# Graph convolution stage on one core: pairs of 64-row products replaced by 128-row products, and four buffers behind the first product

## The chip, the cores and the metric

The kernel runs on 1 core of one Trainium2 chip (trn2). The metric is the device time of one execution in microseconds (us), lower is better. The kernel before takes 10347.91 us, the median of 3 runs (10343.13 to 10349.23).

## The reference, cut to what matters

Four graph layers follow one another on 100000 nodes and 50000 edges with 64 features. The change touches the first layer alone, two "tag convolutions" in a row:

```python
K = 5;  F_IN, F_HID, F_OUT = (64, 128, 64)

def _tag_conv(x, row, col, norm, W, b):
    out = x @ W[0]
    h = x
    for k in range(1, K + 1):
        msg = h[row] * norm[:, None]
        h = jax.ops.segment_sum(msg, col, num_segments=N_NODES)
        out = out + h @ W[k]
    return out + b

h = jax.nn.leaky_relu(_tag_conv(x, row, col, norm, W0, b0), negative_slope=0.01)
h = jax.nn.leaky_relu(_tag_conv(h, row, col, norm, W1, b1), negative_slope=0.01)
```

`W0` is 6 x 64 x 128 and `W1` is 6 x 128 x 64. So for each row of a node that receives edges the first convolution needs six products (x and its five hops, 64 features each) that are added into 128 hidden features, and the second begins with one product of these 128 by all six matrices of `W1` side by side (6 x 64 = 384 columns). The other three layers (a SAGE and GAT layer, a GCN layer, a GAT layer with a dense one) are not touched.

## The kernel before, in words

Edges are sorted by target. They are laid out as 128 partitions by 392 columns, and worked on in NG = 49 groups of 8 columns; a group holds 1024 rows of 64 float32, 256 KB. The first layer runs in four parts. (1) The rows of x are gathered into the table `xc`. (2) Four hop stages: GpSimd (POOL) gathers 8 columns of rows per group, one indirect DMA each (`gather`, L710), VectorE (DVE) weighs them (`feed_vector`, L739) and forms running sums in a ring of three buffers `sums` (L753, L763), SyncE (SP) stores them as the next hop's table. Beside it TensorE (PE) transposes each group into feature-major form, ScalarE (ACT) copies the result (L1056), and SP stores it in the "turned" tables, so that four of the six operands of the first convolution lie in DRAM already turned. Layers for nodes without edges ("dense") run beside these stages and are spread over them by step numbers. (3) The **conv stage**, which the change is about, with no dense work in it: the fifth hop (called `top`) is gathered and summed in the same way, and both the first convolution and the product by `W1` are computed group by group. (4) Five "up" stages, which gather rows of the results y5 to y0 and so form the second convolution.

The order of the conv stage is written out by hand, engine by engine, for a group g:

- SP: `cat_load(g)` (L1286, L1289) loads x from `xc` and the four turned tables into `cat[g % 2]`, five transfers of 256 KB, once the products of group g-2 are done. `y_store(g - 3)` (L1295) then stores six blocks of 256 KB.
- PE, `conv_tensor`: `conv_turn(g, 0)` transposes x (four 128x128 transposes, L1079), `conv_turn(g, 1)` the sums. A partition of such a turned block is 64 features of one column (rows 0 to 63) and 64 of the next (rows 64 to 127). `conv_mult` (L1095) does six steps of two products, each over 64 partitions, 64x128 weights and 512 columns: one for the upper and one for the lower half, into the banks PS[2] and PS[3]. The first waits for `biased`, that is until ACT has emptied these banks from group g-1. Then `conv_out(g - 1)` does 8 products (L1108, 128 partitions by 384 columns) into three banks in turn; product y waits until bank y-3 has been copied out.
- ACT, `conv_scalar`: two copies of transposed blocks (`conv_move`, L1128), then the four even copies out of the product banks (`conv_out_scalar(g - 1)`, L1139), then the bias, two activations (L1156) from PS[2] and PS[3] into the two buffers `hid`. They wait for the products of the first convolution and, since `hid` has two buffers alone, for all 8 products of `conv_out(g - 1)`.
- DVE: `feed_vector(g)`, 8 steps of sums (`paced_sums`), then the four odd copies (`conv_out_vector(g - 3)`, L1146), then the leaky relu of two buffers (`conv_leak(g - 2)`, L1162).
- POOL gathers up to six groups ahead of DVE.

The waits that the change moves are these (L1151 to L1156):

```python
if g:
    conv_out_scalar(e, g - 1)
e.wait_ge(*conv["mult"](K6 * (g + 1)))
e.wait_ge(*conv["product"](K8 * g))
for a in range(2):
    e.activation(hid[a][:, :], PS[2 + a][:, :], ACT.Identity,
```

## Time and profile before

| | |
|---|---|
| time, median of 3 runs | 10347.91 us (10343.13 to 10349.23) |
| the profiled execution: its time, its span | 10350.19 us, 10348.5 us |
| PE busy / weight loads | 5760.6 us (56%) / 2887.3 us (28%) |
| DVE busy | 5897.1 us (57%) |
| ACT busy | 3169.7 us (31%) |
| POOL busy | 6886.8 us (67%) |
| DMA | 1016.84 MB, 98 GB/s on average |
| mean granted TensorE clock | 0.768 |

The busy shares are averages over stages with different limits. PE counts two instructions per float32 product, and for each a weight load that can run beside the product before it. The granted clock is 1.00 at 2.4 GHz and 0.50 at 1.2 GHz. The conv stage runs from about 3205 to 3846 us of the span. How the page and the answers are read: each row of a timeline begins with the start and the length in us, and in brackets stand the idle time of the engine before it and what released it.

### The profile page before, as it was taken

To read this page: it belongs to the slowest core of one execution; us is meant where nothing else is said; L and a number is where in the kernel's file an instruction comes from. 1 tells how busy PE (TensorE), PEld (TensorE's weight loads), DVE (VectorE), ACT (ScalarE), POOL (GpSimd) and SP (SyncE) were. 2 spreads that over 40 slices of the span, in tenths; PEclk is the share of its full clock that TensorE was granted. 3 is DMA by queue.
4 is the path that set the end of the run, shared out by engine and by line. 5 is a ranking of instruction groups with operands and counts; after the bars stand their busy time and mean duration, and the time that the engine had idled before them with its cause. 6 is when DMAs were issued, how large, how long until landed. Compare 5 with 4: busy or idle time off the path is not lost. (4 is left out here: it accounts for less than half of the span.)

```text
span 10348.5 us, 86417 instructions
## 1 busy us (share of the span) xinstructions
PE 5760.6 (56%) x19261; PEld 2887.3 (28%) x19261; DVE 5897.1 (57%) x16861; ACT 3169.7 (31%) x5395; POOL 6886.8 (67%) x6659
## 2 busy tenths in 40 slices
PE   1672465555566984555555400598885776720277
PEld 0331232333333542222222200243222333410143
DVE  2341565556555656666666578544449994520697
ACT  0351233333332322222222201244443553310144
POOL 7777777777777747777777777775750006767477
PEclk9796677777777996676666655799998997755698
DMA  4620332222224752222222222222333442222353
GB/s 130 202 84 20 84 109 89 89 86 92 87 90 156 245 206 83 89 88 85 86 89 86 82 74 80 69 72 57 72 61 111 146 139 63 75 52 52 81 151 121
DMA packets 967572, 1016.84 MB, mean 98 GB/s; under 512 B 530229, under 2 KB 584231, under 8 KB 954507
## 3 DMA queue, kind: packets, MB, share of 16 engines
q1 hardware_dynamic: 754186, 880.78, 26.3%
q0 software_dynamic: 212864, 130.53, 7.1%
q8 instruction: 154, 2.52, 0.1%
q14 instruction: 368, 3.01, 0.1%
HBM read 491.86 MB, written 596.27 MB: 105 GB/s over the span
## 5 line engine op out<-in xcount | busy, mean ns | idle before, releaser
L710 POOL DMA_INDIRECT gathered<-u,place_of_source x1564 | 1645.0, 1052 | 522.5 <-issue 476.3
L710 POOL DMA_INDIRECT gathered<-hop,place_of_source x1564 | 1615.0, 1033 | 530.4 <-issue 492.0
L763 DVE SCALAR_TENSOR_TENSOR first_node_sum<-sums,ends_first,first_node_sum 128x64 f32<-128x64 f32 x4680 | 1302.7, 278 | 8.3 <-DVE sums L753 6.8
L739 DVE TENSOR_TENSOR weighted<-gathered,bank 128x512 f32<-128x512 f32 (+1 forms) x490 | 335.6, 685 | 1407.5 <-DMA gathered<-hop,place_of_source 625.3
L753 DVE SCALAR_TENSOR_TENSOR sums<-sums,same_as_before,weighted 128x64 f32<-128x64 f32 x3900 | 1079.3, 277 | 69.0 <-DVE weighted L739 41.9
L710 POOL DMA_INDIRECT gathered<-x,row_of_source x782 | 806.3, 1031 | 300.0 <-issue 224.0
L480 PE MATMUL bank<-dense_tmp,mean 128*128 128x512 f32 x980 | 569.5, 684 | 37.4 <-ACT dense_tmp L489 31.7
L2187 POOL DMA_INDIRECT out_dram<-lane_out,node_to_write x392 | 407.2, 1039 | 274.5 <-ACT lane_out L2108 160.2
L710 POOL DMA_INDIRECT gathered<-y,place_of_source x391 | 406.8, 1040 | 233.0 <-issue 118.9
L710 POOL DMA_INDIRECT first_sum<-head_sums,row_of_first_end x2 | 2.0, 1025 | 827.9 <-DMA head_sums<-head_sums 827.6
L710 POOL DMA_INDIRECT pair<-h_sage,row_of_source x391 | 404.6, 1035 | 220.5 <-issue 125.6
L459 PE MATMUL bank<-g3pair,dense_yT 128*128 128x16 f32 x784 | 176.1, 304 | 669.2 <-DVE dense_yT L529 669.2
L710 POOL DMA_INDIRECT source_row<-x,row_of_source x391 | 398.6, 1019 | 155.1 <-issue 118.9
L480 PE MATMUL bank<-dense_a,center 128*128 128x512 f32 x588 | 406.3, 781 | 168.5 <-DVE dense_a L504 116.8
L710 POOL DMA_INDIRECT gathered<-in_x_dram,dst_index x392 | 401.2, 1024 | 130.0 <-issue 116.5
L710 POOL DMA_INDIRECT gathered<-x_with_place,src_index x391 | 401.4, 1027 | 120.8 <-issue 118.3
L1030 POOL DMA_INDIRECT x_with_place<-own_place,place_to_write x391 | 396.9, 1015 | 127.2 <-issue 127.2
L491 ACT ACTIVATE dense_a<-bank,v_bl 128x512 f32<-128x512 f32 x196 | 134.7, 687 | 1075.8 <-PE bank L602 860.2
L459 PEld LDWEIGHTS bank<-g3pair,dense_yT 128*128 128x128 f32 x784 | 185.6, 311 | 747.9 <-DVE dense_yT L529 747.9
L2227 DVE SCALAR_TENSOR_TENSOR head_sums<-head_sums,same_as_before 128x256 f32<-128x256 f32 x780 | 379.4, 486 | 22.7
L423 PE MATMUL bank<-ident,dense_xT 128*128 128x128 f32 x392 | 96.6, 393 | 510.1 <-DVE dense_xT L529 510.1
L491 ACT ACTIVATE dense_tmp<-bank,eps_col 128x512 f32<-128x512 f32 x490 | 336.3, 687 | 142.8 <-PE bank L480 141.2
(446 smaller groups left out, 15158.6 us busy)
## 6 DMA issues: line engine op xcount, KB each, us to landing
head_sums<-head_sums SPq DMA_DIRECT2D x98, 1024.0 KB, 4.7
y<-conv_out SPq DMA_DIRECT2D x294, 256.0 KB
conv_out<-y SPq DMA_DIRECT2D x245, 256.0 KB, 3.3
hop<-sums SPq DMA_DIRECT2D x196, 256.0 KB, 2.1
turned<-rows_turned SPq DMA_DIRECT2D x196, 256.0 KB, 2.7
cat<-turned SPq DMA_DIRECT2D x196, 256.0 KB
u<-conv_out SPq DMA_DIRECT2D x196, 256.0 KB, 2.0
lane_raw<-x SPq DMA_DIRECT2D x196, 256.0 KB
```

Source lines behind the costliest of these rows:

```text
L423: m = e.transpose(W.bank[l][0][:, q * P:(q + 1) * P], src_ap(l, q), ident[:])
L459: e.matmul(W.bank[l][1][:, q * 4 * HEADS:(q + 1) * 4 * HEADS], two, wts[w][:], start=True, stop=True)
L480: m = e.matmul(W.bank[l][b][:, :], w, W.b(v, l), start=i == 0, stop=i == len(pairs) - 1)
L491: m = e.activation(W.b(o, l), src_ap, func, bias=v[:, 0:1], scale=scale)
L710: return e.indirect_dma_start(out=into, out_offset=None, in_=tab, in_offset=bass.IndirectOffsetOnAxis(ap=index, axis=0), bounds_check=top, ...
L739: e.tensor_tensor(weighted[g % 2][:, 0:n, :], st.rows_of(g), over(st.weight[:, cols], D), ALU.mult).then_inc(st.weighed.handle, 1)
L753: e.scalar_tensor_tensor(s[:, k, :], b, go[:, t:t + 1], m[:, k, :], ALU.mult, ALU.add).then_inc(st.summed.handle, 1)
L763: e.scalar_tensor_tensor(h, row_, flast[:, t:t + 1], h, ALU.mult, ALU.add).then_inc(st.headed.handle, 1)
L1030: e.indirect_dma_start(out=x66, out_offset=bass.IndirectOffsetOnAxis(ap=place_at[:, t:t + 1], axis=0), in_=own[:, t, :], in_offset=None, b ...
L2187: e.indirect_dma_start(out=out, out_offset=bass.IndirectOffsetOnAxis(ap=scat[:, t:t + 1], axis=0), in_=W.out[0][0][:, k * D:(k + 1) * D], ...
L2227: e.scalar_tensor_tensor(s[:, k, :], b, go[:, t:t + 1], s[:, k, :], ALU.mult, ALU.add).then_inc(summed.handle, 1)
```

## The change

1. The operands of the first product are laid so that a column of 128 partitions holds two tables (hop 1 and 2; hop 3 and 4; x and hop 5) for the same rows: `TWO`, weights `w0two` (three 128x128 blocks). `conv_mult` has three steps of two products over 128 partitions.
2. To get this layout, the turned tables are one DRAM tensor, of which `cat_load` takes four pieces of 64 partitions; x is loaded into `both[g % 3]`, beside the sums of `top`, row for row, so that one set of 8 transposes turns both.
3. `hid` has four buffers; ACT's bias stands ahead of the copies of `conv_out(g - 1)` and waits for `conv_out(g - 2)` alone; DVE does the leaky relu of g-1 right behind the sums of g, and the copies of g-2 behind it.

```diff
-            cat = [sb(ctx, f"cat{i}", [P, HOPS, 512]) for i in range(2)]
-            hid = [sb(ctx, f"hidden{i}", [P, 512]) for i in range(2)]
+            both = [sb(ctx, f"x_and_sums{i}", [P, K8, 2, D]) for i in range(3)]
+            top_sums = [a[:, :, 1, :] for a in both]
+            cat = [sb(ctx, f"cat{i}", [P, 2, 2, 512]) for i in range(2)]
+            hid = [sb(ctx, f"hidden{i}", [P, 512]) for i in range(4)]
...
-            def conv_turn(e, g, i):
-                n = 2 * g + i
-                if i:
-                    e.wait_ge(*top.ended(g))
-                else:
-                    e.wait_ge(*cat_in[g % 2](16 * HOPS * (g // 2 + 1)))
-                if n >= 2:
-                    e.wait_ge(*conv["moved"](n - 1))
-                two = sums[g % 3][:].rearrange("p k d -> p (k d)") if i else cat[g % 2][:, 0, :]
+            def conv_turn(e, g, a):
+                if a == 0:
+                    e.wait_ge(*x_again[g % 3](16 * (g // 3 + 1)))
+                    e.wait_ge(*top.ended(g))
+                if g:
+                    e.wait_ge(*conv["moved"](2 * g + a - 1))
                 for q in range(4):
-                    t = e.transpose(PS[i][:, q * P:(q + 1) * P], two[:, q * P:(q + 1) * P], ident[:])
+                    t = e.transpose(PS[a][:, q * P:(q + 1) * P], both[g % 3][:, 2 * q + a, :, :].rearrange("p s d -> p (s d)"), ident[:])
                 t.then_inc(conv["turned"].handle, 1)
...
-                    half = slice(a * D, (a + 1) * D)
-                    t = e.matmul(PS[2 + a][:, :], wts["w0pair"][half, k, :], rhs[half, :], start=m == 0, stop=m == HOPS)
+                    n = 2 * g + a
+                    if m == 2:
+                        e.wait_ge(*conv["moved"](n + 1))
+                    rhs = turned_t[n % 4][:, :] if m == 2 else cat[g % 2][:, m, a, :]
+                    t = e.matmul(PS[2 + a][:, :], wts["w0two"][:, m, :], rhs, start=m == 0, stop=m == 2)
...
-                for m in range(HOPS + 1):
+                for m in range(3):
                     conv_mult(e, g, m)
...
+                e.wait_ge(*conv["mult"](3 * (g + 1)))
+                if g >= 2:
+                    e.wait_ge(*conv["product"](K8 * (g - 1)))
+                for a in range(2):
+                    e.activation(hid[2 * (g % 2) + a][:, :], PS[2 + a][:, :], ACT.Identity,
+                                 bias=wts["v_b0"][:, 0:1]).then_inc(conv["biased"].handle, 1)
                 if g:
                     conv_out_scalar(e, g - 1)
-                e.wait_ge(*conv["mult"](K6 * (g + 1)))
-                e.wait_ge(*conv["product"](K8 * g))
-                for a in range(2):
-                    e.activation(hid[a][:, :], PS[2 + a][:, :], ACT.Identity,
-                                 bias=wts["v_b0"][:, 0:1]).then_inc(conv["biased"].handle, 1)
...
+                    tables = turned.rearrange("(m s g a f) c -> s g f m a c", m=2, s=2, g=NG, a=2)
                     def cat_load(g):
+                        if g >= 3:
+                            e.wait_ge(*conv["turned"](2 * (g - 2)))
+                        e.dma_start(both[g % 3][:, :, 0, :], columns(xc, g)).then_inc(x_again[g % 3].handle, 16)
                         if g >= 2:
-                            e.wait_ge(*conv["mult"](K6 * (g - 1)))
-                        e.dma_start(cat[g % 2][:, 0, :].rearrange("p (k d) -> p k d", d=D), columns(xc, g)
-                                    ).then_inc(cat_in[g % 2].handle, 16)
-                        for m in range(1, HOPS):
-                            e.dma_start(cat[g % 2][:, m, :], ttab[m - 1][g * P:(g + 1) * P, :]).then_inc(cat_in[g % 2].handle, 16)
+                            e.wait_ge(*conv["mult"](3 * (g - 1)))
+                        for m in range(2):
+                            for s in range(2):
+                                e.dma_start(cat[g % 2][s * D:(s + 1) * D, m, :, :], tables[s, g, :, m, :, :]).then_inc(cat_in[g % 2].handle, 16)
...
-                        paced_sums(e, top, g, sums[g % 3], sums[(g - 1) % 3], none, 0, 0, False)
-                        if g >= 3:
-                            conv_out_vector(e, g - 3)
+                        paced_sums(e, top, g, top_sums[g % 3], top_sums[(g - 1) % 3], none, 0, 0, False)
+                        if g:
+                            conv_leak(e, g - 1)
                         if g >= 2:
-                            conv_leak(e, g - 2)
-                    conv_out_vector(e, NG - 3)
-                    conv_leak(e, NG - 2)
-                    fix_vector(e, top, sums[(NG - 1) % 3])
+                            conv_out_vector(e, g - 2)
+                    fix_vector(e, top, top_sums[(NG - 1) % 3])
+                    conv_leak(e, NG - 1)
                     conv_out_vector(e, NG - 2)
-                    conv_leak(e, NG - 1)
                     conv_out_vector(e, NG - 1)
```

ACT in the middle of the conv stage, one group, before (`rows_turned` are the copies of transposed blocks, `conv_out` the copies out of the product banks):

```order
L1128 COPY rows_turned_1<-bank 128x512 [waits conv_mult,conv_turned] x2
L1139 COPY conv_out_1<-bank 128x6x64 [waits conv_product,y_stored1]
L1139 COPY conv_out_1<-bank 128x6x64 [waits conv_product] x3
L1156 ACTIVATE hidden_1<-bank,v_b_1 128x512 [waits conv_product,conv_mult]
L1156 ACTIVATE hidden_1<-bank,v_b_1 128x512
```

and with the change:

```order
L1129 COPY rows_turned_1<-bank 128x512 [waits conv_mult,conv_turned] x2
L1156 ACTIVATE hidden_1<-bank,v_b_1 128x512 [waits conv_product,conv_mult]
L1156 ACTIVATE hidden_1<-bank,v_b_1 128x512
L1140 COPY conv_out_1<-bank 128x6x64 [waits conv_product,y_stored1]
L1140 COPY conv_out_1<-bank 128x6x64 [waits conv_product] x3
```

The two activations moved from behind the four copies to ahead of them.

DVE there, from the end of one group's sums to the beginning of the next, before:

```order
L763 SCALAR_TENSOR_TENSOR first_node_sum<-sums_1,ends_first,first_node_sum 128x64 [waits first_added,summed]
L1146 COPY conv_out_1<-bank 128x6x64 [waits conv_product,y_stored0]
L1146 COPY conv_out_1<-bank 128x6x64 [waits conv_product] x3
L1162 SCALAR_TENSOR_TENSOR hidden_1<-hidden_1 128x512 [waits conv_biased] x2
L739 TENSOR_TENSOR weighted_1<-gathered_1,bank 128x512 [waits gathered0]
```

and with the change:

```order
L765 SCALAR_TENSOR_TENSOR first_node_sum<-x_and_sums_1,ends_first,first_node_sum 128x64 [waits first_added,summed]
L1165 SCALAR_TENSOR_TENSOR hidden_1<-hidden_1 128x512 [waits conv_biased] x2
L1147 COPY conv_out_1<-bank 128x6x64 [waits conv_product,y_stored1]
L1147 COPY conv_out_1<-bank 128x6x64 [waits conv_product] x3
L741 TENSOR_TENSOR weighted_1<-gathered_1,bank 128x512 [waits gathered4]
```

The leaky relu moved from behind the four copies to ahead of them, and a group's sums are followed by the relu of the group before it.

PE there, from the transposes to the first product by `w1cat`, before:

```order
L1079 MATMUL bank<-ident,cat_1 128x128 [waits conv_moved,cat_loaded0]
L1079 MATMUL bank<-ident,cat_1 128x128 x3
L1079 MATMUL bank<-ident,sums_1 128x128 [waits conv_moved,summed]
L1079 MATMUL bank<-ident,sums_1 128x128 x3
L1095 MATMUL bank<-cat_1,w0pair 128x512 [waits conv_biased]
L1095 MATMUL bank<-cat_1,w0pair 128x512 x7
L1095 MATMUL bank<-rows_turned_1,w0pair 128x512 [waits conv_moved]
L1095 MATMUL bank<-rows_turned_1,w0pair 128x512
```

and with the change:

```order
L1082 MATMUL bank<-ident,x_and_sums_1 128x128 [waits conv_moved,summed,x_in1]
L1082 MATMUL bank<-ident,x_and_sums_1 128x128 x3
L1082 MATMUL bank<-ident,x_and_sums_1 128x128 [waits conv_moved]
L1082 MATMUL bank<-ident,x_and_sums_1 128x128 x3
L1096 MATMUL bank<-cat_1,w0two 128x512 [waits conv_biased,cat_loaded1]
L1096 MATMUL bank<-cat_1,w0two 128x512 x3
L1096 MATMUL bank<-rows_turned_1,w0two 128x512 [waits conv_moved] x2
```

Both transposes now wait for the sums; the wait for the loaded tables moved to the first product; six products stand where twelve stood.

## Rows read from the trace of the kernel before

**Rows 1.** Windows view: us; busy (count) of PE, PEld, DVE, ACT, POOL; clock, DMA, GB/s.

```profile
3440.00:3540.00 100.00, 95.66 (x398) 50.73 (x396) 60.44 (x186) 34.57 (x67) 77.44 (x75) 1.00 0.74 247
```

**Rows 2.** Timeline of one group in mid-stage, PE's rows.

```profile
3502.64 0.60 PE L1079 MATMUL bank<-ident,cat 128*128 128x128 f32 x4
3503.07 0.60 PE L1079 MATMUL bank<-ident,sums 128*128 128x128 f32 x4
3504.22 3.70 PE L1095 MATMUL bank<-cat,w0pair 64*128 64x512 f32 x16 [0.54 <-ACT hidden L1156]
3507.75 1.88 PE L1095 MATMUL bank<-rows_turned,w0pair 64*128 64x512 f32 x8
3509.57 4.81 PEld L1108 LDWEIGHTS bank<-w1cat,hidden 128*128 128x128 f32 x16 [0.76 <-issue]
3509.57 5.43 PE L1108 MATMUL bank<-w1cat,hidden 128*128 128x384 f32 x16
3514.83 0.60 PE L1079 MATMUL bank<-ident,cat 128*128 128x128 f32 x4
```

**Rows 3.** The same timeline, rows of ACT and DVE.

```profile
3502.90 1.27 ACT L1156 ACTIVATE hidden<-bank,v_b 128x512 f32<-128x512 f32 x2 [0.23 <-PE bank L1108]
3503.62 1.29 DVE L1162 SCALAR_TENSOR_TENSOR hidden<-hidden 128x512 f32<-128x512 f32 x2 [0.22 <-ACT hidden L1156]
3504.05 1.07 ACT L1128 COPY rows_turned<-bank 128x512 f32<-128x512 f32 x2
3504.83 0.68 DVE L739 TENSOR_TENSOR weighted<-gathered,bank 128x512 f32<-128x512 f32 x1
3508.62 0.27 DVE L763 SCALAR_TENSOR_TENSOR first_node_sum<-sums,ends_first,first_node_sum 128x64 f32<-128x64 f32 x1
3510.57 0.48 ACT L1139 COPY conv_out<-bank 128x384 f32<-128x384 f32 x1 [5.44 <-PE bank L1108]
3511.23 0.56 DVE L1146 COPY conv_out<-bank 128x384 f32<-128x384 f32 x1 [2.34 <-PE bank L1108]
3515.03 0.56 DVE L1146 COPY conv_out<-bank 128x384 f32<-128x384 f32 x1 [0.73 <-PE bank L1108]
```

**Rows 4.** Timeline, then windows view, of dense work: full 128-row products of 512 columns.

```profile
571.36 1.02 PE L610 MATMUL bank<-dense_xT,w 128*128 128x512 f32 x2
572.22 1.02 PE L480 MATMUL bank<-dense_a,center 128*128 128x512 f32 x2
...
570.00:578.00 8.00, 6.94 (x16) 2.43 (x14) 2.76 (x5) 6.18 (x11) 6.17 (x7) 1.00 0.25 78
```

**Rows 5.** Timeline of PE's weight loads: the last 64-row pairs of the group.

```profile
3508.18 0.19 PEld L1095 LDWEIGHTS bank<-rows_turned,w0pair 64*128 64x128 f32 x2 [0.24 <-issue]
3508.61 0.19 PEld L1095 LDWEIGHTS bank<-rows_turned,w0pair 64*128 64x128 f32 x2 [0.23 <-issue]
```

**Rows 6.** Timeline, the first groups of the stage.

```profile
3242.63 1.28 DVE L1162 SCALAR_TENSOR_TENSOR hidden<-hidden 128x512 f32<-128x512 f32 x2
3248.84 0.69 DVE L739 TENSOR_TENSOR weighted<-gathered,bank 128x512 f32<-128x512 f32 x1 [4.93 <-DMA gathered<-hop,place_of_source]
3253.37 5.26 PE L1108 MATMUL bank<-w1cat,hidden 128*128 128x384 f32 x8 [4.56 <-DVE conv_out L1146]
3270.94 0.60 PE L1079 MATMUL bank<-ident,cat 128*128 128x128 f32 x4
```

**Rows 7.** Timeline, the end of the stage.

```profile
3733.81 1.00 POOL L710 DMA_INDIRECT gathered<-hop,place_of_source  x1 [0.30 <-issue]
3836.01 5.43 PE L1108 MATMUL bank<-w1cat,hidden 128*128 128x384 f32 x16 [2.16 <-DVE hidden L1162]
```

**Rows 8.** DMA view, 3340 to 3640 us: packets, MB, share of 16 engines.

```profile
q1 hardware_dynamic: 38967, 70.97, 68.4%
q0 software_dynamic: 7075, 2.64, 4.9%
```

**Rows 9.** DMA view, 340 to 500 us.

```profile
q1 hardware_dynamic: 48277, 29.99, 59.8%
x_placed<-in_x_dram SPq DMA_DIRECT2D x36, 256.0 KB, 3.4
```

More of the change, by code:

```diff
@@ L125, in bass_gnn_resnorm @@
     hop = [xc] + [dram(f"hop{k}", (RP, D)) for k in range(1, HOPS)]
-    ttab = [dram(f"turned{k}", (NG * P, 512)) for k in range(1, HOPS)]
+    turned = dram("turned", ((HOPS - 1) * NG * P, 512))
     ytab = [dram(f"y{k}", (RP, D)) for k in range(HOPS + 1)]
@@ L159, in bass_gnn_resnorm @@
         wts[n] = sb(stack, n, [P, P])
-    for n, shape in (("w00", [P, 2, P]), ("w10", [P, 2, P]), ("w0pair", [P, HOPS + 1, P]), ("w1cat", [P, HOPS + 1, D]),
+    for n, shape in (("w00", [P, 2, P]), ("w10", [P, 2, P]), ("w0two", [P, (HOPS + 1) // 2, P]), ("w1cat", [P, HOPS + 1, D]),
                      ("gl_stack", [P, 2, 2, P]), ("g3_stack", [P, 2, 2, P]), ("glz", [P, W4]),
@@ L221, in load_weights @@
             put(wts["v_b0"][:, :], col(b0))
-            for lo in (0, D):
-                put(wts["w0pair"][lo:lo + D, :, :], W0.rearrange("k f m -> f k m"))
+            for m, two in enumerate(TWO):
+                for s, k in enumerate(two):
+                    put(wts["w0two"][s * D:(s + 1) * D, m, :], W0[k, :, :])
             put(wts["w1cat"][:, :, :], W1.rearrange("k f m -> f k m"))
```

40 lines of the change are left out of this document (17 added, 23 removed).

## The prediction

> **What bounds the kernel now.** The page puts POOL, DVE and PE at 56 to 67% of the span, which says nothing of one stage, so I read the stage first in the windows view. In the conv stage PE is busy 95.66 of 100 us at a granted clock of 1.00; POOL, the next, 77.44 with 75 gathers, and DVE 60.44 [rows 1]. POOL issues a gather every 100 / 75 = 1.333 us, so a group of 8 costs it 10.67 us. Its last gather begins at 3733.81, while PE works on until 3841.44 [rows 7]: the gathers have run ahead, and PE sets the end. The timeline then gives PE's period: the transposes of one group begin at 3502.64 and those of the next at 3514.83, 12.19 us apart [rows 2]. It splits into three pieces: 1.58 us for 8 transposes and a wait, until the first product at 3504.22; 5.35 us for the twelve 64-row products, until 3509.57; 5.26 us for the 8 products by `w1cat` [rows 2]. In the first piece the four transposes take 0.43 us each time, 0.86 together, and the other 0.72 is the wait for ACT: the bias begins at 3502.90, as soon as the eighth product of the group before is done, lasts 1.27, and PE goes on 0.05 later [rows 2, 3].
>
> **The products.** This is where the words "six for twelve" could mislead. PE loads the weights of the 64-row products in twos, 0.43 us apart, at 3508.18 and 3508.61 [rows 5]. Twelve products are 24 instructions, 16 of them in the row that begins at 3504.22 [rows 2], so 12 such twos, 12 x 0.43 = 5.16 us: an instruction for the upper half and one for the lower share the 0.43 us. A product over all 128 rows with 512 columns, at the same clock of 1.00, begins 0.86 us before the next [rows 4], 0.43 per instruction. Six of them are 6 x 0.86 = 5.16 us, as long as the twelve. What goes is the change-over between the two shapes: the first weights of `w1cat` begin only at 3509.57, after 0.76 us without a load, where 3508.61 + 0.43 would have been in step [rows 2, 5]. Of that I count 5.35 - 5.16 = 0.19 us ahead of the products by `w1cat`, and 0.19 inside them, the unhidden first weight load: DVE copies every second product, and its first and fourth copy begin at 3511.23 and 3515.03 [rows 3], so two products take 1.267 us, one 0.634, eight 5.07 instead of 5.26.
>
> The Trainium skill says in "TensorE: Matmul & The Clock Gate", "Step-by-step: what each phase is for", that a product takes as many cycles as it has columns, whatever its rows. Taken alone, this halves the products' time, which is a rival below.
>
> **The period after the change.** Transposes 0.86, six products 5.16, eight products 5.07: 11.09 us if nobody waits. The wait for the bias goes, since ACT does the bias of a group right behind its products, while PE does the products by `w1cat` of the group before. But that puts 1.15 us of ACT (3502.90 to the next copy at 3504.05) and 1.21 us of DVE (3503.62 to 3504.83) [rows 3] exactly where both must empty the three product banks. Let T be the start of the products by `w1cat`, 0.634 us each. ACT begins the bias at T + 0.23 [rows 3] and so the copy of product 0 at T + 1.38 instead of T + 0.87, done at T + 1.86. Product 3, due at T + 1.90, wants this bank, PE's reaction of 0.05 and a weight load of 0.19 us [rows 5]: T + 2.10, 0.20 late. DVE begins the relu 0.72 us behind the bias [rows 3], at T + 0.95, so its copy of product 1 begins at T + 2.16 and ends at T + 2.72; product 4 begins at T + 2.96 instead of T + 2.73, 0.23 more. The later copies catch up, each having 1.27 us for 0.48 or 0.56. So 0.43 us come back and the **period is 11.52 us**. Ends: 0 if both gaps close, and 0.86 if each delay is twice what I have. Value taken: 0.43, from rows of the same engines in the same stage.
>
> **What lies beside other work.** DVE's new order leaves sums only one group ahead of PE instead of two. From its last copy (starting 0.2 us after PE's turn to the transposes, 0.56 long) weighing and sums last 4.07 us (3504.83 to 3508.89 [rows 3]), about 4.8 us after the transposes began; the relu can start at 0.86 + 5.16 + 0.95 = 6.97. That is 2.1 us of cover; without it every us of delay would be one of the period. The gathers (10.67) stay below 11.52. The same 8 sums, copies, two bias and two relu instructions are done as before. The later start of the x transposes, now behind the sums, costs nothing for the same reason. SP issues 11 transfers per group as before. x lands in pieces of 256 bytes now, since it is interleaved with the sums: 1024 packets for 128. Packets of the hardware queue take 0.684 x 16 x 300 / 38967 = 0.084 us in this stage [rows 8]. In a stretch where 36 loads of x land in such pieces, 48277 packets take 0.598 x 16 x 160 / 48277 = 0.032 us on average; 36864 of them are the small ones, and with 0.084 for the rest, 0.0155 is left for one [rows 9]. So the x load goes from 128 x 0.084 / 16 = 0.67 us of all 16 engines to 1024 x 0.0155 / 16 = 0.99 (2.03 at the average of 0.032). The DMA engines are busy 73.6% of 12.19 = 8.97 us per group with both queues and the rest [rows 8]; 9.29 of 11.52 stay below the period. The weights' four more small loads at the start, and the waits no longer needed ahead of the first sums, I cost at 0: nothing waits for the SP queue there, and the gathers pace the first sums.
>
> **Head and tail.** Before, group 0's products by `w1cat` stalled: leaky relu 0 came after the sums of group 2 (3242.63), and the odd copies of group 0 after the sums of group 3, for whose gathers DVE waited until 3248.84; PE went on at 3253.37, at half speed (8 instructions in 5.26 us against 16 in 5.43), and reached the end of group 1's at 3270.94 [rows 2, 6]. With the change relu 0 lies before the sums of group 2 and copy 1 right behind relu 1: 3242.63 + 1.21 + 0.56 = 3244.4, four products more and PE turns to group 2 at 3247.2. One period later, plus 1.5 us because the clock will have fallen in the wait (an estimate from the half speed just named), gives 3260.2 where 3270.94 stood: 10.7 us. At the end the last relu no longer waits for copies, and PE's idle 2.16 us before the last products go [rows 7]; four transposes more behind the last sums cost 0.4: 1.8 us.
>
> **Sum.** 45 periods from there to the last groups by 12.19 - 11.52 = 0.67 us: 30.2. With head and tail: 30.2 + 10.7 + 1.8 = 42.7 us. The stages behind only start earlier. Against the profiled execution (10350.19 us, 1.7 more than its span) this is 10307.5; the median of the runs is 2.3 lower, so the forecast is **10305.2 us**. Bounds: with no collision 45 x 0.43 = 19.4 less, 10286; with 0.86, 19.4 more, 10325.
>
> **The rivals.**
> - *No collision* (0.12): the copies slip into gaps, period 11.09, about 10286. For it: each bank has slack, the collision is a matter of 0.2 us each time. Against: both engines wait for the same product end.
> - *Collision twice as large* (0.14): period 11.95, about 10325. For it: three banks and two copiers give little reserve.
> - *Half the time for the products* (0.03): PE about 9 us a group (11.52 - 2.58); then the gathers set the end. Last gather 3733.8, sums 4 us, about 25 us for the rest: 3763 instead of 3841, 10270. Against: [rows 4, 5].
> - *A new wait for each old one* (0.04): `leak` or the gathers' landing holds PE each period, which stays near 12.1; 10348 less the 4 us of 45 x 0.09 and a few of the head: about 10338.
> - *The DMA engines become the bound* (0.07), the slower side. The tables are loaded in four pieces of 64 partitions. If such a packet takes twice 0.084, 512 of them add 512 x 0.084 / 16 = 2.69 us; with x at 2.03, the sum is 8.97 - 0.67 + 2.03 + 2.69 = 13.0 us a group. It decides from 11.52 on, and in place of 12.19 it costs 45 x 0.8 = 36, less 12 of head and tail: 10372. Against: no row has packets that slow, and with either one of the prices alone the sum is 12.0 or 10.3. For it: the engines are at 74% already, in bursts. The Trainium skill has this rule in "SBUF — State Buffer", "Door 1: The DMA port swizzle": partitions 0 to 63 reach only 8 of 16 ports. No row of this trace shows a large transfer of 64 partitions.
>
> **How the numbers follow.** The forecast's own case has 0.60. A measurement of this kernel can tell 0.2%, 20.7 us, from no change, so 10327.2 and 10368.6 are the borders. The forecast, no collision, most of the twice as large one, and halved products are faster: 0.60 + 0.12 + 0.09 + 0.03, rounded to 0.83. The other 0.05 of the twofold collision, the new waits and a mild DMA bound give 0.11 for no change; 0.06 is slower. The range reaches from 10283, just below the case without collision, to 10332, over the twofold one; left out are halved products, new waits and the DMA bound, some 0.14, and a rest.
>
> **What would show it.** PE's period between transposes 11.5 to 11.6 us; the six products 0.86 apart, 5.16 to 5.2 together (2.6 would be the halving); no idle time of the product L1096 for ACT, but short idle times of L1109 for ACT and DVE in products 3 and 4, 0.4 us a group together; no gap in the weight loads at the change from L1096 to L1109; ACT's bias 0.2 us behind the products; the conv stage's DMA share near 0.80 and not above 0.9; the end of the last product near 3799 instead of 3841. If the DMA share goes to 0.95 or more, or DVE waits for gathers all through the stage, the prediction is wrong.

## The result, and the profile after

The changed kernel takes **10303.39 us**, the median of 6 runs (10294.09 to 10310.46), against 10346.78 us (10343.13 to 10349.23, 6 runs) for the kernel before on the same chip: ratio 0.9957, 95% interval 0.9944 to 0.997. That is 0.43% faster and 1.8 us from the forecast. The profiled execution took 10302.5 us with a span of 10300.8 us; the span before was 10348.5, 47.7 us more.

The windows view of the changed kernel, of the stretch of [rows 1], with the same columns:

```profile
3440.00:3540.00 100.00, 100.00 (x312) 51.98 (x311) 63.42 (x201) 35.78 (x69) 77.38 (x75) 1.00 0.96 263
```

PE has no idle time left that this view shows, where it had 4.34 us in 100. The count of its instructions fell from 398 to 312, and yet it is not less busy: one 128-row instruction costs what two of 64 rows did. The last three numbers are the clock, still 1.00, the share of the DMA engines, which rose from 0.74 to 0.96, and the GB/s.

The timeline of one group, PE's rows and after them those of ACT and DVE, answers to [rows 2] and [rows 3]. Line numbers moved a little: L1082 are the transposes, L1096 the products of the first convolution, L1109 those by `w1cat`, L1156 and L1165 bias and relu, L1140 and L1147 the copies of ACT and DVE.

```profile
3506.19 1.04 PE L1082 MATMUL bank<-ident,x_and_sums 128*128 128x128 f32 x8
3507.07 3.60 PE L1096 MATMUL bank<-cat,w0two 128*128 128x512 f32 x8
3510.50 1.88 PE L1096 MATMUL bank<-rows_turned,w0two 128*128 128x512 f32 x4
3511.36 0.19 PEld L1096 LDWEIGHTS bank<-rows_turned,w0two 128*128 128x128 f32 x1 [0.24 <-issue]
3511.79 0.19 PEld L1109 LDWEIGHTS bank<-w1cat,hidden 128*128 128x128 f32 x1 [0.24 <-issue]
3512.22 5.59 PE L1109 MATMUL bank<-w1cat,hidden 128*128 128x384 f32 x16
3512.42 1.27 ACT L1156 ACTIVATE hidden<-bank,v_b 128x512 f32<-128x512 f32 x2 [4.51 <-PE bank L1096]
3513.14 1.29 DVE L1165 SCALAR_TENSOR_TENSOR hidden<-hidden 128x512 f32<-128x512 f32 x2 [2.27 <-ACT hidden L1156]
3513.58 0.48 ACT L1140 COPY conv_out<-bank 128x384 f32<-128x384 f32 x1
3514.11 0.30 PEld L1109 LDWEIGHTS bank<-w1cat,hidden 128*128 128x128 f32 x2 [0.41 <-ACT conv_out L1140]
3514.35 0.55 DVE L1147 COPY conv_out<-bank 128x384 f32<-128x384 f32 x1
3514.96 2.23 PEld L1109 LDWEIGHTS bank<-w1cat,hidden 128*128 128x128 f32 x8 [0.55 <-DVE conv_out L1147]
3517.64 1.04 PE L1082 MATMUL bank<-ident,x_and_sums 128*128 128x128 f32 x8
```

The period is 3517.64 - 3506.19 = 11.45 us in place of 12.19, in three pieces: 0.88 (transposes, no wait), 5.15 (six products), 5.42 (the eight by `w1cat`). The first product follows the transposes at once. At 3511.36 and 3511.79 the weight loads pass from L1096 to L1109 in step, 0.43 apart, where 0.76 us without a load stood. The price is to be seen at 3514.11 and 3514.96: two weight loads of L1109 wait for the first copy of ACT and the first of DVE, which now stand behind bias and relu. The waits view over the stage (3240 to 3780 us; total us, times, longest) says that this happens in every group; apart from these two, PE waits for another engine only once there, 3.6 us in the stage's head:

```profile
PEld bank L1109 <- DVE conv_out L1147: 29.7, 47, 4.3
PEld bank L1109 <- ACT conv_out L1140: 19.1, 47, 0.4
```

The DMA view of 3340 to 3640 us, as in [rows 8]:

```profile
q1 hardware_dynamic: 65651, 75.55, 88.7%
q0 software_dynamic: 7142, 2.66, 5.6%
```

Start and end of the stage, in the timeline, answer to [rows 6] and [rows 7]:

```profile
3205.55 1.09 PE L1051 MATMUL bank<-ident,sums 128*128 128x128 f32 x4 [0.44 <-ACT rows_turned L1062]
3225.11 0.69 DVE L741 TENSOR_TENSOR weighted<-gathered,bank 128x512 f32<-128x512 f32 x1 [19.15 <-DMA gathered<-hop,place_of_source]
3243.67 2.80 PE L1109 MATMUL bank<-w1cat,hidden 128*128 128x384 f32 x8
3250.11 4.38 PE L1109 MATMUL bank<-w1cat,hidden 128*128 128x384 f32 x8 [3.64 <-DVE conv_out L1147]
3265.77 1.04 PE L1082 MATMUL bank<-ident,x_and_sums 128*128 128x128 f32 x8
...
3788.03 10.75 PE L1109 MATMUL bank<-w1cat,hidden 128*128 128x384 f32 x32
```

**Where the 47.7 us of the span came from.** Groups are counted from 0. From the transposes of group 3 to those of the last group (48) are 45 periods: 3270.94 to 3820.19 before and 3265.77 to 3781.98 now, 549.2 and 516.2 us, so 33.0 us are gained. 44 of them took 12.20 us on average and take 11.45; the last one was 12.37 and is 12.45, so it brings nothing. Up to group 3 the changed kernel is at 3265.77 instead of 3270.94: 5.2. The last products end at 3798.78 instead of 3841.44, which leaves 4.5 for the tail. The stages behind took 5.0 us less (10300.8 - 3798.78 against 10348.5 - 3841.44); that is less than runs of one kernel differ by, and I have no cause for it.

### The profile page after: what moved, and what is told of

It is laid out like the page before. It is cut to its first block and busy times, and to the rows that moved or that the text cites. A ratio compares the mean times of both kernels' runs of the same rounds, so it can differ in the third digit from the quotient of the medians.

```text
span 10300.8 us, 85241 instructions
## 1 busy us (share of the span) xinstructions
PE 5743.3 (56%) x18673; PEld 2877.3 (28%) x18673; DVE 5894.6 (57%) x16861; ACT 3169.3 (31%) x5395; POOL 6882.6 (67%) x6659
## 3 DMA queue, kind: packets, MB, share of 16 engines
q1 hardware_dynamic: 797770, 880.58, 27.4%
## 5 line engine op out<-in xcount | busy, mean ns | idle before, releaser
L765 DVE SCALAR_TENSOR_TENSOR first_node_sum<-sums,ends_first,first_node_sum 128x64 f32<-128x64 f32 x4290 | 1204.1, 281 | 7.6 <-DVE sums L755 6.3
L755 DVE SCALAR_TENSOR_TENSOR sums<-sums,same_as_before,weighted 128x64 f32<-128x64 f32 x3510 | 980.8, 279 | 63.4 <-DVE weighted L741 41.0
L712 POOL DMA_INDIRECT first_sum<-head_sums,row_of_first_end x2 | 2.0, 1024 | 831.6 <-DMA head_sums<-head_sums 830.9
```

The costliest lines, as they stand in the source:

```text
L712: return e.indirect_dma_start(out=into, out_offset=None, in_=tab, in_offset=bass.IndirectOffsetOnAxis(ap=index, axis=0), bounds_check=top, ...
L755: e.scalar_tensor_tensor(s[:, k, :], b, go[:, t:t + 1], m[:, k, :], ALU.mult, ALU.add).then_inc(st.summed.handle, 1)
L765: e.scalar_tensor_tensor(h, row_, flast[:, t:t + 1], h, ALU.mult, ALU.add).then_inc(st.headed.handle, 1)
```

## The experiments

The theory: PE sets the period; the change takes away PE's wait for the bias and the changes of shape, gives a part back where bias and relu stand ahead of the first copies, and the DMA engines, though nearly full by their share, bind nothing. The main rival: DMA sets the 11.45 us.

No later run had a chip like the first one. On the four chips of these runs the kernel before takes 12128 to 12258 us instead of 10347, so the table shows two things: the ratio on that chip, and the period between the groups that run undisturbed, which can be compared across chips, since these periods agree (before 12.2 and after 11.45 on either). "Stage" is the time from the first to the last transposes of the conv stage. Period and stage come from one profiled execution each.

| kernel | time, us | before, same chip | ratio, 95% interval | period | stage |
|---|---|---|---|---|---|
| before, first chip | 10346.78 | | | 12.19 | 605.9 |
| changed, first chip | 10303.39 | 10346.78 | 0.9957 (0.9944 to 0.997) | 11.45 | 553.1 |
| before_control (kernel before) | 12174.46 | 12127.58 | one run | 12.2 | 704.8 |
| after_again (changed) | 12163.78 | 12137.97 | 1.0019 (1.0004 to 1.0034) | 11.45 | 716.8 |
| order_only | 12293.56 | 12258.33 | 1.0035 (1.0013 to 1.0056) | 11.66 | 759.1 |
| products_only | 12248.46 | 12258.33 | 0.9993 (0.9975 to 1.0012) | 12.05 | 682.8 |
| tables_128 | 12281.42 | 12258.33 | one run | 11.45 | 738.2 |
| x_whole | 12305.47 | 12258.33 | one run | 11.44 | 762.5 |
| copies_first | 12157.86 | 12137.97 | 1.0022 (1.0004 to 1.004) | 11.19 | 737.7 |
| copies_first_laid_out | 12176.97 | 12137.97 | 1.0037 (1.0022 to 1.0052) | 11.19 | 720.2 |
| the same, laid_out_again | 12315.88 | 12252.89 | 1.006 (1.0039 to 1.008) | 11.2 | 755.1 |
| the same, laid_out_third | 12177.07 | 12127.58 | 1.0042 (1.0025 to 1.0058) | 11.2 | 728.7 |
| stores_more | 12171.57 | 12137.97 | one run | 11.45 | 731.6 |
| the same, stores_more_again | 12213.86 | 12252.89 | one run | 11.45 | 749.1 |

### The two halves of the change, each alone

order_only is the kernel before with part 3 of the change, products_only the changed kernel without it:

```diff
# order_only, against the kernel before (DVE likewise)
-            hid = [sb(ctx, f"hidden{i}", [P, 512]) for i in range(2)]
+            hid = [sb(ctx, f"hidden{i}", [P, 512]) for i in range(4)]
...
-                if g:
-                    conv_out_scalar(e, g - 1)
...
-                e.wait_ge(*conv["product"](K8 * g))
+                if g >= 2:
+                    e.wait_ge(*conv["product"](K8 * (g - 1)))
...
+                if g:
+                    conv_out_scalar(e, g - 1)
# products_only, against the changed kernel: the same lines the other way round
```

> The kernel before with the four buffers and the new order of ACT and DVE alone; the twelve 64-row products, the loads and the 128-partition tables stay. My theory: the wait for the bias (0.72 us a group) goes, the collision of bias and relu with the first copies (0.35 us in the changed kernel) comes, and the two changes of product shape (0.19 and 0.19) stay, so PE's period is 12.19 - 0.72 + 0.35 = 11.8 us and the whole about 10347 - 46 x 0.37 - 5 to 9 for head and tail = 10321 to 10326. The rival, that six full products are what saves time and the order nothing, expects a period of 12.1 to 12.2 and 10340 or more. DMA share of the stage: as before, 8.97 / 11.8 = 0.76.

> The changed kernel with two hidden buffers and the order of ACT and DVE of the kernel before; six products over 128 rows and the new loads stay. My theory: only the changes of shape go, 0.19 + 0.19 us; the bias wait stays (1.58 us from the first transpose to the first product), 5.16 and 5.07 for the products: period 11.8 us, whole about 10347 - 45 x 0.38 = 10330, at most 3 either way for the head. The rival, that full products take half the time of the pairs, expects 2.6 us for the six and a period bound by the gathers, 10.7, about 10270.

PE's timeline of order_only, where no pause disturbs it:

```profile
4811.61 0.60 PE L1079 MATMUL bank<-ident,cat 128*128 128x128 f32 x4
4812.05 0.60 PE L1079 MATMUL bank<-ident,sums 128*128 128x128 f32 x4
4812.57 3.70 PE L1095 MATMUL bank<-cat,w0pair 64*128 64x512 f32 x16
4816.11 1.88 PE L1095 MATMUL bank<-rows_turned,w0pair 64*128 64x512 f32 x8
4817.93 5.50 PE L1108 MATMUL bank<-w1cat,hidden 128*128 128x384 f32 x16
4823.27 0.60 PE L1079 MATMUL bank<-ident,cat 128*128 128x128 f32 x4
```

and of products_only:

```profile
4305.77 1.04 PE L1082 MATMUL bank<-ident,x_and_sums 128*128 128x128 f32 x8
4307.44 3.67 PE L1096 MATMUL bank<-cat,w0two 128*128 128x512 f32 x8 [0.63 <-ACT hidden L1157]
4310.95 1.88 PE L1096 MATMUL bank<-rows_turned,w0two 128*128 128x512 f32 x4
4312.66 5.32 PE L1109 MATMUL bank<-w1cat,hidden 128*128 128x384 f32 x16
4317.82 1.04 PE L1082 MATMUL bank<-ident,x_and_sums 128*128 128x128 f32 x8
```

| us | transposes and wait | first products | by `w1cat` | period |
|---|---|---|---|---|
| before | 1.58 | 5.35 | 5.26 | 12.19 |
| products_only | 1.67 | 5.22 | 5.16 | 12.05 |
| order_only | 0.96 | 5.36 | 5.34 | 11.66 |
| changed | 0.88 | 5.15 | 5.42 | 11.45 |

The order brings 0.53 of the 0.74 us by itself, the products 0.14 by themselves and 0.21 on top of the order. Both expectations had 11.8 us and missed it, in opposite directions. In order_only the products by `w1cat` are only 0.08 us longer than before, not 0.35. In products_only the changes of shape give back 0.13 and 0.10 us, not 0.19 twice, and the piece with the bias wait is 0.09 us longer. Both rivals are refuted all the same: the order is not worth nothing, and full products are not half as long.

Twelve products of 64 rows, two at a time, or six products of 128 rows are 5.16 us of work either way; what differs is the change of shape: 5.36 and 5.35 us up to the products by `w1cat` against 5.15 and 5.22. The part of the change that its description leads with is the small one.

### The collision: copies ahead of bias and relu

```diff
# copies_first: ACT copies 0, 2 and 4, then the bias, then 6; DVE copies 1, 3 and 5, then the relu, then 7
+                if g:
+                    conv_out_scalar(e, g - 1, (0, 2, 4))
...
                 if g:
-                    conv_out_scalar(e, g - 1)
+                    conv_out_scalar(e, g - 1, (6,))
... (DVE likewise)
```

> The changed kernel, but ACT copies products 0, 2 and 4 out before it does the bias and 6 behind it, and DVE copies 1, 3 and 5 before the leaky relu and 7 behind it. My theory: the 0.35 us a group that PE waits in the products by w1cat goes, the period is 11.09 to 11.12 instead of 11.45, the whole 46 x 0.35 = 16 us faster than the changed kernel, 10287 on a chip with 10347 before. The rival: the DMA engines, busy 10.9 us a group, are full at this period (98%), transfers land late, and the period stays above 11.3 with PE or DVE waiting for stores or loads.

The period falls to 11.19 us, and PE's products by `w1cat` have no wait left. The rows are those of copies_first_laid_out (below), which has the same order and period:

```profile
4728.86 5.32 PE L1111 MATMUL bank<-w1cat,hidden 128*128 128x384 f32 x16
4729.76 0.48 ACT L1142 COPY conv_out<-bank 128x384 f32<-128x384 f32 x1 [4.04 <-PE bank L1111]
4732.66 1.27 ACT L1160 ACTIVATE hidden<-bank,v_b 128x512 f32<-128x512 f32 x2
4733.41 1.28 DVE L1169 SCALAR_TENSOR_TENSOR hidden<-hidden 128x512 f32<-128x512 f32 x2
4734.02 1.04 PE L1084 MATMUL bank<-ident,x_and_sums 128*128 128x128 f32 x8
```

From 4728.86 to 4734.02 are 5.16 us for the eight products. So the collision costs 5.42 - 5.16 = 0.26 us a group, less than the 0.35 that I expected to get back; the period was expected at 11.09 to 11.12. The rival of this run, full DMA engines and a period above 11.3, is refuted.

### What the loads cost the DMA engines

tables_128 takes the tables in full rows of 128 partitions (the first product then gets other rows of them; its output isn't the convolution). x_whole loads x in pieces of 2 KB into a buffer of its own, and ACT lays it beside the sums.

```diff
# tables_128
-                                e.dma_start(cat[g % 2][s * D:(s + 1) * D, m, :, :], tables[s, g, :, m, :, :]).then_inc(cat_in[g % 2].handle, 16)
+                                t = (2 * m + s) * NG + g
+                                e.dma_start(cat[g % 2][:, m, s, :], turned[t * P:(t + 1) * P, :]).then_inc(cat_in[g % 2].handle, 16)
# x_whole (waits left out)
...
+                e.copy(both[g % 3][:, :, 0, :], sums[g % 3][:, :, :]).then_inc(x_laid.handle, 1)
...
-                        e.dma_start(both[g % 3][:, :, 0, :], columns(xc, g)).then_inc(x_again[g % 3].handle, 16)
+                        e.dma_start(sums[g % 3][:, :, :], columns(xc, g)).then_inc(x_again[g % 3].handle, 16)
```

> The changed kernel, but each of the four table loads fills all 128 partitions from one block of 128 rows, as before; bytes and number of 2 KB packets are the same. The first product thereby gets other rows, so the output is not the layer's; only the loads' speed is asked. The stage's DMA share was 0.95 where I had 0.81 worked out, 10.9 us of all 16 engines per group instead of 9.3. If packets into 64 partitions are the slow ones, the share falls to about 9.3 / 11.45 = 0.81 here; if it is the 256-byte packets of x, it stays at 0.95. The period stays 11.45 in both.

> The changed kernel, but x is loaded in 2 KB rows into a buffer of its own and ACT lays it beside the sums (one copy of about 0.6 us per group, in ACT's idle time). If the 256-byte packets are the slow ones, the DMA share falls from 0.95 to about 8.97 / 11.45 = 0.78, a small packet having cost (10.88 - 8.30) x 16 / 1024 = 0.040 us; if it is the half-partition loads, it falls only by 0.03, to 0.92. The period stays 11.45 in both. The head of the stage, where DVE waited for the first gathers until 3225.1 (19.6 us after the last hop's transposes, before: 15.4), goes back by up to 4 us if the small packets stood in the gathers' way.

The hardware queue in the DMA view, 4200 to 4700 us, of order_only, tables_128, products_only and x_whole in this order:

```profile
q1 hardware_dynamic: 53136, 96.75, 55.5%
```

```profile
q1 hardware_dynamic: 85050, 98.64, 60.2%
```

```profile
q1 hardware_dynamic: 96891, 112.78, 79.2%
```

```profile
q1 hardware_dynamic: 51594, 93.94, 63.0%
```

A group has 1584 packets of this queue before the change (38967 over 300 / 12.19 groups in [rows 8]), and 1584 - 128 + 1024 = 2480 with x in small pieces. That gives the number of groups in each window, and with the gathers' queue (3.9, 4.2, 4.6 and 4.1%) the time of a group's packets, spread over the 16 engines: order_only 59.4% x 500 / 33.5 = 8.9 us, tables_128 9.4, products_only 10.7, x_whole 10.3. On the first chip it is 8.9 before and 94.3% x 11.45 = 10.8 after. Three prices follow. Small pieces of x alone (order_only to tables_128) cost 0.5 us. Loads of 64 partitions alone (tables_128 to products_only, or to the changed kernel on the first chip) cost 1.3 to 1.4 us, so a packet of such a load takes 1.4 x 16 / 512 = 0.044 us more than the 0.084 of the others, half as much again. And none of them sets the period: with 9.4 us (tables_128), 10.3 (x_whole) and 10.8 (the changed kernel) it stays at 11.45, 11.44 and 11.45.

The same loads are what delays the stage's first sums. DVE's first weighing in the stage and its wait for the gathered rows, in the timelines of order_only, tables_128, x_whole and products_only:

```profile
4080.91 0.69 DVE L739 TENSOR_TENSOR weighted<-gathered,bank 128x512 f32<-128x512 f32 x1 [15.19 <-DMA gathered<-hop,place_of_source]
```

```profile
4087.79 0.69 DVE L741 TENSOR_TENSOR weighted<-gathered,bank 128x512 f32<-128x512 f32 x1 [15.94 <-DMA gathered<-hop,place_of_source]
```

```profile
4097.76 0.69 DVE L741 TENSOR_TENSOR weighted<-gathered,bank 128x512 f32<-128x512 f32 x1 [18.44 <-DMA gathered<-hop,place_of_source]
```

```profile
4074.54 0.69 DVE L741 TENSOR_TENSOR weighted<-gathered,bank 128x512 f32<-128x512 f32 x1 [19.27 <-DMA gathered<-hop,place_of_source]
```

On the first chip the wait was 14.95 us before and is 19.15 now. In tables_128 full rows take 3.3 us of it away; whole pieces of x take 0.8, though there the first load of x also waits for the stores of the last hop. In the three runs of copies_first_laid_out, which has full rows too, the wait is 17.1 to 17.3 us, so the gain there is about 2. These first loads and gathers run at one time; that the slow loads hold up the gathers is my reading of these waits.

The Trainium skill, in "SBUF — State Buffer", "Door 1: The DMA port swizzle", says that 64 partitions reach only 8 of 16 ports. The direction is borne out here: 0.128 us for a packet of such a load instead of 0.084. A plain doubling, which the rival of the prediction had taken, is not, in a stream where other transfers run beside these.

### Both mended, and the engines loaded further

copies_first_laid_out also writes the turned tables into DRAM so that a load of 128 partitions finds the two tables one below the other:

```diff
-                e.dma_start(turned[(n * NG + g) * P:(n * NG + g + 1) * P, :], turned_t[u % 4][:, :]).then_inc(rows_kept[u % 4].handle, 16)
+                for a in range(2):
+                    to = ((n // 2 * NG + g) * 2 + a) * P + n % 2 * D
+                    e.dma_start(turned[to:to + D, :], turned_t[u % 4][a * D:(a + 1) * D, :]).then_inc(rows_kept[u % 4].handle, 16)
...
-                            for s in range(2):
-                                e.dma_start(cat[g % 2][s * D:(s + 1) * D, m, :, :], tables[s, g, :, m, :, :]).then_inc(cat_in[g % 2].handle, 16)
+                            for a in range(2):
+                                e.dma_start(cat[g % 2][:, m, a, :], tables[g, :, m, a, :]).then_inc(cat_in[g % 2].handle, 16)
```

> As copies_first, and the turned tables are stored in DRAM so that each load fills all 128 partitions (the hop stages' stores go out as two transfers of 64 partitions instead of one). My theory: DMA time per group falls from 10.8 to 9.4 us, as with tables_128, share 9.4 / 11.1 = 0.85, period 11.09 to 11.12, whole 10284 to 10288; the hop stages have DMA shares of 0.2 to 0.4 and don't feel two smaller stores. If DMA was what held copies_first, this one is the faster of the two by up to 10 us; if not, they are within 3 us.

> The changed kernel, but each group stores the first two of its six result blocks a second time into spare tables: 512 KB more per group, 256 packets of 2 KB, 256 x 0.084 / 16 = 1.34 us of all 16 engines. My theory: 10.8 + 1.34 = 12.2 us per group is more than PE's 11.45, the DMA engines are the bound, period 12.1 to 12.4 at a share of 0.98 or more and about 10303 + 46 x 0.75 = 10338. The rival, that the share of 0.95 overstates what is used and there is room, expects the period to stay at 11.45.

copies_first_laid_out has 9.3 us of DMA a group (62.2 + 4.4% in its window) and the same 11.19 as copies_first. stores_more is the changed kernel with two of the six blocks of y stored a second time, into spare tables (+256 packets a group); 84% of 500 us over 35.3 groups is 11.9 us of DMA per group on average, and the undisturbed groups still take 11.45. Both kernels were run again on a further chip, with the same periods. The pauses described next could give the queue time to catch up, but they end before the stage does. The windows view of stores_more_again from there on, columns as in [rows 1]:

```profile
4700.00:4790.00 90.00, 90.00 (x285) 47.11 (x285) 56.45 (x176) 32.75 (x64) 22.71 (x22) 1.00 1.03 300
```

PE is busy throughout, and seven groups in a row are 11.45 us apart (transposes at 4708.69 and 4788.82), for each of which the packets take 1.03 x 11.45 = 11.8 us of 16 engines. stores_more shows the same at its end (1.04 of 4720 to 4740). So the theory stated for this run, 12.1 to 12.4 us a group, fails and its rival stands as far as seven groups can tell: a share above 1.00 is more than engines that do one packet after the other could have, so the times of packets overlap, and a share of 0.95 doesn't say that only 5% is left. What load would bind was not reached.

### Why the later chips show no gain

> The changed kernel itself, unaltered, as the control of this call. The first call's chip ran the kernel before at 12258 us instead of 10347, with ACT idle for long stretches that the profile puts to 'remote'; there the order alone gave 1.0035 and the products alone 0.9993. On a chip that runs the kernel before at about 10347 I expect 10303 (0.9957) and a period of 11.45 us. On one that runs it at about 12258 my theory expects the period of 11.45 between ACT's delays but a whole that is no faster, 0.995 to 1.005, since each delay of ACT now falls on PE twice a group or so; the rival, that only the new order suffers there, expects 1.003 or more.

The unaltered changed kernel has the 11.45 us again, but in the main only every other group. The distances between its transposes read 11.4 17.0 11.9 11.4 18.4 11.5 15.1 11.4 15.8 and so on. PE, ACT and SP's queue in such a group:

```profile
4307.82 2.10 PE L1109 MATMUL bank<-w1cat,hidden 128*128 128x384 f32 x6
4309.75 2.54 SPq L1295 DMA_DIRECT2D cat<-turned  x4
4309.76 1.27 ACT L1156 ACTIVATE hidden<-bank,v_b 128x512 f32<-128x512 f32 x2 [4.54 <-remote]
4311.95 0.91 PE L1109 MATMUL bank<-w1cat,hidden 128*128 128x384 f32 x2 [2.04 <-issue]
4314.18 5.49 PE L1109 MATMUL bank<-w1cat,hidden 128*128 128x384 f32 x8 [1.31 <-issue]
```

PE had gone on from the products that the bias waits for to those by `w1cat` at 4307.82. On the first chip ACT follows 0.2 us behind that point, here 1.94 us, with a releaser that the profile calls "remote", which names no wait in the two profiles of the first chip. The first copy, behind the bias, then starts only at 4311.42, and PE stops after six instructions. SP's load of the next tables waits for the same products, and it starts in the same moment. From 4200 to 4700 us that is so in all 35 groups, to 0.01 us, whether both are 0.2 us behind PE or up to 8.0. So it is not ACT that is slow: what comes late is PE's signal, to both that wait for it. The pauses end some seven groups before the stage does: in after_again the last long group ends at 4683, POOL's last gather starts at 4694.37, and in between and after it each group takes 11.4 again. The old order seemed to be spared most of this in products_only, so the kernel before was profiled there as well:

> The kernel before, unaltered, under the profile on the chip of this call. Theory (the later chips' pauses go with the gathering, and the old order covers most of them): if the kernel before takes some 12100 to 12300 us here, undisturbed groups are 12.19 us apart as before, long groups are rare (about one in ten, like products_only), and the stage takes 680 to 700 us from its first transposes to its last, less than the 717 us of the changed kernel (after_again). Rival (the pauses hit every kernel alike): a pause every other group here too, 12.19 instead of 11.45 between them, and the stage takes some 750 us. If the chip is like the first one (10350 us), 12.19 throughout and 606 us.

Behind the stage's head it reads 12.2 nearly throughout, with three groups of 21 to 22 us, and 704.8 us for the stage against 716.8 for the changed kernel. Two single executions 12 us apart prove little, since the stage of copies_first_laid_out alone went from 720 to 755; but from group 2 on the two kernels with the old order take 594 (before_control) and 586 us (products_only), the ten runs with one of the new orders 630 to 675. On the first chip it was 562 before and is 528 now. In before_control ACT is late too, in 28 groups of some 38, but ahead of copies that no one waits for at once:

```profile
ACT rows_turned L1128 <- remote: 35.0, 28, 1.4
```

(the waits view of before_control, 4200 to 4700 us). So the theory stated for this run held, with the stage 5 us longer than its band: the chips differ, and the old order lets most late starts pass unseen while the new one does not. That the reason is the slack (bias and relu of a group now stand directly behind its products, and DVE is one group nearer to PE) fits these rows, but no run varied it. products_only, which keeps the old order, has the shortest stage of all on those chips. The head is another matter. On the later chips group 2's transposes come 70 to 94 us after group 1's with either order (93.7 in before_control, 69.9 in after_again), on the first 27.4 before and 17.5 now; in after_again PE's signal reaches ACT and SP 24 us late there, at 4126.14. Of the 99 us that the stage of the kernel before loses, 66 are lost in the head. What delays the signals there stays open: that the pauses stop about when the gathers do was seen in each of the runs with the new order, but no run took the gathers away.

> Four copies ahead of the bias and the relu, tables laid out for loads of 128 partitions, once more. On a chip where the kernel before takes about 10350 us: groups 11.19 us apart, 45 x 0.26 = 12 us below the changed kernel's 10303, so about 10291 us, ratio 0.9945. Rival: the copies ahead bring a new wait, 10303 or more. On a chip where the kernel before takes some 12200 us: ratio 1.003 to 1.006 as before.

(It is three copies of each engine that stand ahead, six of eight.) It met such a chip once more: 12177.07 against 12127.58 us, ratio 1.0042 (1.0025 to 1.0058), 11.2 us between pauses, stage 728.7. Whether it beats the changed kernel on a chip like the first, by the 45 x 0.26 = 12 us that its period promises, was not to be measured.

## Why the prediction was right, point by point

The forecast of 10305.2 us met 10303.39. The mechanism held: PE sets the end, its wait for the bias goes, and the collision takes a part back. But five terms were off in size, some too high and some too low, and that the medians come within 1.8 us of the forecast is luck: in the profiled pair it is 5.0 off.

- **Bound, and six for twelve: right.** PE set the end before and does after. The six products take 5.15 us, weight loads 0.43 apart, where I had 5.16. Halving is refuted, since the 64-row products already ran two at a time. The Trainium skill has in "TensorE: Matmul & The Clock Gate", "Step-by-step: what each phase is for", that the columns set the time; the trace agrees, 0.43 us for an instruction of 128 rows as for a pair of 64. In "TensorEngine Tiling (Array Packing)", "Key Properties", the Trainium skill says that tiles of the array work independently and that a change of mode drains it; that fits the pairs of [rows 5] and the 0.76 us without a load in [rows 2].
- **Changes of shape: size off.** I counted 0.19 + 0.19 us; products_only shows 5.35 - 5.22 = 0.13 and 5.26 - 5.16 = 0.10. The second came from reading 5.07 us for eight products out of the distance of DVE's copies; without any wait they take 5.16 (products_only and copies_first_laid_out).
- **The bias wait: right.** 0.72 expected; 1.58 - 0.88 = 0.70 measured.
- **The collision: mechanism right, size off.** Both waits stand where I put them, in both engines, and every group has them. They cost 0.26 us, not 0.43: I had added the two delays in full. The profile's waits, 0.41 and 0.55, are those of the weight loads, which run beside the product before and so overstate PE's loss. Unstalled products 0.09 too short and a collision 0.17 too long leave 0.08, with the other pieces 0.07: the period of 11.52 became 11.45. That is the 2.8 us between 30.2 and 33.0: 45 x 0.07 = 3.2, some 0.7 more because before's periods averaged 12.21 and not 12.19, and 1.0 less because the last period is 12.45.
- **DMA: the term that failed.** I expected 9.29 us per group and a share of 0.80, and wrote that 0.95 would make the prediction wrong. The share is 0.94 to 0.96, so by my own sign it was. In the sum of the forecast the 64-partition loads cost nothing extra ("no row has packets that slow"); they cost 1.4 us, x 0.5 instead of 0.32: 8.97 + 0.5 + 1.4 = 10.9 of 11.45. The rival had that half right, but its other half, that the time of the packets becomes the period once it is the longer one, is wrong up to 11.8 us at least, as stores_more_again shows. My sign rested on the same step and was wrong for the same reason. The period came out right because DMA was not its bound at all.
- **Head: 5.2 instead of 10.7.** The hop stage ahead of it ended 2.1 us later (3205.55 for 3203.47), for which I have no cause; the first sums came 4.2 us later still, 2 to 3.3 of it by the slow loads, as the runs above suggest; the rest of the head went 0.8 us better than I had it. The loads can be seen in the DMA views of the two heads, in 40 slices of 0.675 us from 3203 on, of before

```profile
GB/s 0 115 385 385 370 385 300 20 143 361 343 197 268 350 367 358 358 402 393 356 133 10 20 0 19 0 15 0 17 0 19 0 15 0 20 2 14 7 8 10
```

  and of after:

```profile
GB/s 0 0 0 0 82 379 385 382 388 325 20 131 264 257 252 253 197 219 256 205 175 217 238 164 244 218 243 209 236 187 204 99 16 19 0 15 0 20 0 15
```

  The loads ran at some 350 to 400 GB/s in most slices and ended about slice 20; now they run mostly at 160 to 260 until slice 31. I had costed the loads of the head at 0, which goes back to the same mis-sized term.
- **Tail: 4.5 instead of 1.8.** PE's idle time before the last products is gone as said (2.3 us); the last 32 instructions follow one another (10.75 us). Another 0.2 is the change of shape. The other 2.0 us lie in the last transposes, which I had 0.4 us dearer: before, PE waited between the two sets for the last sums,

```profile
3822.48 0.66 PE L1079 MATMUL bank<-ident,sums 128*128 128x128 f32 x4 [1.69 <-DVE sums L768]
```

  and now both sets stand behind these sums, so that this wait lies ahead of them, in the last period, and is part of what made it 12.45 us.
- **Behind the stage** 5.0 us less than the "only start earlier" of the forecast.

Sum: 33.0 + 5.2 + 4.5 + 5.0 = 47.7 against 30.2 + 10.7 + 1.8 = 42.7 in the profiled pair; the medians, 43.4 apart, are nearer to the forecast than its terms are.

## What to carry to other kernels

Count the work of packed products from the distance between their weight loads before merging them: where pairs already share the array, merging buys the change-over alone (here 0.14 to 0.21 us of 12). When a layout is got by loading half the partitions, price these loads from a run; here the packets of such a load take half as much again, which costs where transfers come in a burst (2 to 3.3 us at the stage's head) before it shows in the period. Don't take a DMA share of 0.95 for a bound: here 1.03 left the period as it was; load the engines further and look. An order with work of two groups interleaved more tightly was faster where every signal came at once and lost where some came late: time it on more than one chip.

## What was unexpected of the hardware

Chips differ: one ran the kernel before in 10347 us, the four others in 12128 to 12258 us, at a mean granted clock of about 0.73 against 0.77. In the conv stage the clock is not what differs (undisturbed groups take the same time to 0.01 us); signals that come 1 to 8 us late do, and 24 us late in the head. On the one of these chips where it was timed, the same change that gave 0.43% costs 0.19% (0.04 to 0.34). The DMA share of the profile can pass 1.00, and PE loses nothing at 1.03. Further, 256-byte pieces of a load cost little, some (0.52 + 0.67) x 16 / 1024 = 0.019 us each against 0.084 for one of 2 KB, so that the packets of a load in eight times as many pieces take less than twice as long.
